# Block-diagonal queries and keys laid out by 24 small copies within SBUF for each batch, in place of masked products on POOL

## What is computed

```python
Q = (x @ Wq + bq).reshape(B, S, H, Hd)            # H = 16 heads, Hd = 16
K = (x @ Wk + bk).reshape(B, S, H, Hd)
scores = jnp.einsum('bqhd,bkhd->bhqk', Q, K) * scale + alibi
attn = softmax(scores, axis=-1)                   # self: over the keys
...
sm = jnp.einsum('nlhd,nshd->nlhs', q, k) / math.sqrt(D)
sm = softmax(sm, axis=1)                          # cross: over the queries
attn = jnp.einsum('nlhs,nshd->nlhd', sm, v)
...
x = layernorm(x + ffn(x))                         # quantised weights and activations
```

## Time and profile before

| | before |
|---|---|
| median of 3 runs | 1400.16 us (1396.43 to 1400.56) |
| the profiled execution, its own time | 1398.15 us |
| its span (first to last instruction) | 1396.4 us |
| PE busy | 1226.5 us (88%) |
| PE weight loads | 897.2 us (64%) |
| DVE busy | 1159.4 us (83%) |
| ACT busy | 859.7 us (62%) |
| POOL busy | 396.4 us (28%) |
| the core's 16 DMA engines | 24 GB/s mean |
| TensorE clock granted, mean | 0.966 of full |

### The profile page before, as it was taken

How to read it: one execution, slowest core, us unless ns; L and a number is a source line. 1 busy time by engine, 2 the same in 40 slices (tenths; PEclk the granted TensorE clock), 3 DMA queues, 4 the chain that set the end, 5 groups by cost and what they waited for, 6 DMA issues and landing times. The chain is left out here.

```text
span 1396.4 us, 28360 instructions
## 1 busy us (share of the span) xinstructions
PE 1226.5 (88%) x8850; PEld 897.2 (64%) x8850; DVE 1159.4 (83%) x2358; ACT 859.7 (62%) x2306; POOL 396.4 (28%) x463
## 2 busy tenths in 40 slices
PE   1689999999999999999999999999858878596776
PEld 1466666666666666666666666666527766496776
DVE  6369999999999999999999999999853468868787
ACT  2366666666666666666666666666424479786443
POOL 0233322234322234322234322233100000000887
PEclk9999999999999999999999999999969989798898
DMA  5100000000000000000000000000000000000222
GB/s 159 39 19 16 19 28 25 18 21 18 18 27 22 18 21 18 18 28 21 18 21 18 18 29 21 19 19 5 7 7 1 0 0 0 0 1 8 62 69 72
DMA packets 35042, 33.07 MB, mean 24 GB/s; under 512 B 4148, under 2 KB 34604, under 8 KB 34988
## 3 DMA queue, kind: packets, MB, share of 16 engines
q1 hardware_dynamic: 32704, 31.50, 7.3%
q10 hardware_dynamic: 2284, 0.89, 0.3%
HBM read 25.04 MB, written 7.34 MB: 23 GB/s over the span
## 5 line engine op out<-in xcount | busy, mean ns | idle before, releaser
L561 ACT ACTIVATE Px<-score 125x896 f32<-125x896 f32 x192 | 176.2, 918 | 128.1 <-PE score L1080 66.7
L747 DVE TENSOR_REDUCE nmax_c<-score 125x8 f32<-125x896 f32 x192 | 208.3, 1085 | 5.6 <-PE score L1002 5.1
L729 DVE TENSOR_REDUCE Zc<-Px 125x8 f32<-125x896 f32 x192 | 206.6, 1076 | 7.3 <-ACT Px L561 3.8
L554 ACT ACTIVATE Ps<-score,nmax_s 112x112 f32<-112x112 f32 x512 | 173.1, 377 | 3.9 <-DVE nmax_s L754 3.9
L506 POOL TENSOR_TENSOR rstd<-vare,half 112x1 f32<-112x1 f32 x64 | 35.1, 548 | 473.6 <-DVE vare L839 473.6
L1080 PE MATMUL score<-sel,nmaxT 128*125 128x448 f32 x384 | 125.1, 407 | 1.8 <-ACT nmaxT L567 1.8
L554 ACT ACTIVATION_READ_ACCUMULATOR Ps<-score,nmax_s 112x1 f32 x512 | 118.6, 232 | 0.0
L1091 PE MATMUL outX<-Px,Vn 125*32 125x224 f32 x1536 | 113.2, 368 | 2.5 <-DVE Vn L740 2.5
L740 DVE TENSOR_TENSOR Vn<-Vx,rZc 125x128 f32<-125x128 f32 x192 | 112.8, 588 | 1.2
L567 ACT ACTIVATE nmaxT<-maxT 128x125 fp32r<-128x125 f32 x192 | 53.5, 279 | 89.2 <-PE maxT L1074 88.9
L1002 PE MATMUL score<-Qbd_hi,KxT_hi 64*125 64x448 f32 x384 | 90.3, 466 | 1.2 <-ACT Px L561 1.2
(11 more groups left out here) (252 smaller groups left out, 3588.1 us busy)
## 6 DMA issues: line engine op xcount, KB each, us to landing
ctx_in<-in_ctx SPq DMA_DIRECT2D x32, 375.0 KB
x_in<-in_x SPq DMA_DIRECT2D x32, 112.0 KB, 2.0
x_scratch<-x SPq DMA_DIRECT2D x32, 112.0 KB, 5.4
x2T_all<-x_scratch SPq DMA_DIRECT2D x32, 112.0 KB, 2.0
out<-x2T_all SPq DMA_DIRECT2D x32, 112.0 KB, 1.9
raw_w_up<-in_w_up SPq DMA_DIRECT2D x1, 768.0 KB, 5.6
raw_w_down<-in_w_down SPq DMA_DIRECT2D x1, 768.0 KB, 7.2
raw_w_gate<-in_w_gate SPq DMA_DIRECT2D x1, 768.0 KB, 9.6
```

What stands on the lines that cost most here:

```text
L554: ins = act.activation(Ps[:, g, :], score[slot][0:L, h // QUAD, (h % QUAD) * L:(h % QUAD + 1) * L], ACT.Exp, bias=nmax_s[:, g:g + 1], accu ...
L561: act.activation(Px[u % 2][:].rearrange("s (q h) l -> s q (h l)", q=2), score[SLOT_OF[f"C{u}"]][0:C, :, 0:QW], ACT.Exp).then_inc(exp_c, 1)
L729: dve.tensor_reduce(Zc[p][:], Px[p][:], AX.X, ALU.add).then_inc(z_c, 1)
L747: dve.tensor_reduce(nmax_c[u % 2][:, 0:OCT].rearrange("s (q h) -> s q h", q=2), score[SLOT_OF[f"C{u}"]][0:C, :, 0:QW].rearrange("s q (h l) ...
```

## The change

The kernel after the change makes the same two layouts by plain copies from SBUF to SBUF, issued on SP's queue. One copy moves the 16 partitions of one head slot `(q, j)` to block `j`: for the keys both tiles and both parts at once (8 copies a batch, each 16 x 4 rows of 112 values), for the queries one tile with both parts (8 copies for each tile, each 16 x 2 rows of 112 values). Both tensors are cleared once at the start by POOL, and SP waits for that before its first load of the attention part. `Kbd` now exists twice (by parity of the batch); `Qbd` still exists once. `mask4` and POOL's products are gone. PE waits for all eight key copies of a batch before its first self scores, and for the eight query copies of tile `t` before the first unit of that tile. Source tensors of the high and the low part become halves of one tensor, which moves no work.

```diff
         @block.sync
+            def head_rows(q, j):
+                first = HALF_ROWS * q + HD * j
+                return slice(first, first + HD)
+
+            def diagonal_keys(n):
+                wait_drain(sp, (n, "Ks"))
+                for q in range(2):
+                    for j in range(QUAD):
+                        rows = head_rows(q, j)
+                        sp.dma_start(Kbd_both[n.par][rows, :, :, j].bitcast(F32).rearrange("r p t l -> r (p t) l"),
+                                     Ks_both[rows].bitcast(F32).rearrange("r p t l -> r (p t) l")).then_inc(kbd_done, 16)
+
+            def diagonal_queries(n, t):
+                if t == 0:
+                    wait_drain(sp, (n, "Qx"))
+                else:
+                    wait(sp, scores_c, n.times(NU))
+                for q in range(2):
+                    for j in range(QUAD):
+                        rows = head_rows(q, j)
+                        sp.dma_start(Qbd_both[rows, :, t, j].bitcast(F32), Qx_both[rows, :, t].bitcast(F32)).then_inc(qbd_done[t], 16)
+
+            sp.wait_ge(diagonal_cleared, 3)
+
             def step(n0, n1, n2, n3, n4, n5, n6):
+                if n4:
+                    diagonal_keys(n4)
+                if n2:
+                    diagonal_queries(n2, 0)
                 if n5:
                     load_x(n5)
+                if n2:
+                    diagonal_queries(n2, 1)
+                if n5:
                     load_ctx(n5)
                 if n0:
                     save_x2(n0)
...
         @block.gpsimd
+            for both in (*Kbd_both, Qbd_both):
+                pool.memset(both[:].bitcast(F32), 0.0).then_inc(diagonal_cleared, 1)
             pool.wait_ge(const_ld, constants.LOADED)
-            pool.tensor_tensor(mask4[:], mask8[:, 0:QUAD], mask8[:, QUAD:OCT], ALU.add).then_inc(mask_done, 1)
...
-            def block_diagonal(dst, src, t, done):
-
-                for h in range(2):
-                    ins = pool.tensor_tensor(
-                        dst[h][:, t],
-                        src[h][:, t:t + 1, :].bitcast(F32).broadcast_to([P, QUAD, L]),
-                        mask4[:].rearrange("p (h o) -> p h o", o=1).broadcast_to([P, QUAD, L]), ALU.mult)
-                ins.then_inc(done, 1)
...
             def step(n0, n1, n2, n3, n4, n5, n6):
                 if n5:
                     add_output_bias(n5)
-                if n4:
-                    diagonal_queries(n4, 0)
                 if n2:
                     inverse_root(n2, 1)
-                if n6:
-                    diagonal_keys(n6, 0)
-                    diagonal_keys(n6, 1)
-                if n4:
-                    diagonal_queries(n4, 1)
...
         @block.tensor
             def self_scores(n, t):
-                pe.wait_ge(kbd_done, n.times(KT, t + 1))
+                pe.wait_ge(kbd_done, n.times(HEADS_LAID, HEADS_LAID))
...
             def cross_scores(n, u):
                 if c == 0:
-                    pe.wait_ge(qbd_done, n.times(KT, t + 1))
+                    pe.wait_ge(qbd_done[t], n.times(HEADS_LAID, HEADS_LAID))
```

More of the change, by code:

```diff
@@ L37 @@
 HALF_ROWS = QUAD * HD
+HEADS_LAID = 16 * OCT
 BANK = 512
@@ L181, in __init__ @@
         mask8 = sb("mask8", [P, OCT])
-        mask4 = sb("mask4", [P, QUAD])
         even_odd = sb("even_odd", [P, 2])
@@ L344, in attention @@
         Vx = [sb(f"Vx{p}", [C, NC, D]) for p in range(2)]
-        Qx = [sb(f"Qx_{p}", [P, KT, L], F32R) for p in ("hi", "lo")]
-        Qbd = [sb(f"Qbd_{p}", [P, KT, QUAD, L], F32R) for p in ("hi", "lo")]
+        Qx_both = sb("Qx_both", [P, 2, KT, L], F32R)
+        Qx = [Qx_both[:, p] for p in range(2)]
+        Qbd_both = sb("Qbd_both", [P, 2, KT, QUAD, L], F32R)
+        Qbd = [Qbd_both[:, p] for p in range(2)]
         Qs = [sb(f"Qs_{p}", [P, KT, L], F32R) for p in ("hi", "lo")]
-        Ks = [sb(f"Ks_{p}", [P, KT, L], F32R) for p in ("hi", "lo")]
-        Kbd = [sb(f"Kbd_{p}", [P, KT, QUAD, L], F32R) for p in ("hi", "lo")]
+        Ks_both = sb("Ks_both", [P, 2, KT, L], F32R)
+        Ks = [Ks_both[:, p] for p in range(2)]
+        Kbd_both = [sb(f"Kbd_both{b}", [P, 2, KT, QUAD, L], F32R) for b in range(2)]
+        Kbd = [[both[:, p] for p in range(2)] for both in Kbd_both]
         xT = sb("xT", [P, KT, L])
@@ L395, in attention @@
         ctx_hi, kx_hi, ks_hi, qs_hi, qx_hi = (sem(n) for n in ("ctx_hi", "kx_hi", "ks_hi", "qs_hi", "qx_hi"))
-        kbd_done, qbd_done = sem("kbd_done"), sem("qbd_done")
+        kbd_done, qbd_done = sem("kbd_done"), [sem(f"qbd_done{t}") for t in range(KT)]
         scores_s, nmax_s_done, exp_s = sem("scores_s"), sem("nmax_s_done"), sem("exp_s")
@@ L476, in _ @@
             pool.memset(xmax_all[:], 0.0).then_inc(consts, 1)
+            for both in (*Kbd_both, Qbd_both):
+                pool.memset(both[:].bitcast(F32), 0.0).then_inc(diagonal_cleared, 1)
             pool.wait_ge(const_ld, constants.LOADED)
-            pool.tensor_tensor(mask4[:], mask8[:, 0:QUAD], mask8[:, QUAD:OCT], ALU.add).then_inc(mask_done, 1)
-            pool.wait_ge(mask_done, 1)
             pool.wait_ge(bo_folded, 1)
-            def block_diagonal(dst, src, t, done):
-                for h in range(2):
-                    ins = pool.tensor_tensor(
-                        dst[h][:, t],
-                        src[h][:, t:t + 1, :].bitcast(F32).broadcast_to([P, QUAD, L]),
-                        mask4[:].rearrange("p (h o) -> p h o", o=1).broadcast_to([P, QUAD, L]), ALU.mult)
-                ins.then_inc(done, 1)
-            def diagonal_keys(n, t):
-                if t == 0:
-                    wait_drain(pool, (n, "Ks"))
-                wait(pool, scores_s, n.back(1).times(KT, t + 1))
-                block_diagonal(Kbd, Ks, t, kbd_done)
-            def diagonal_queries(n, t):
-                if t == 0:
-                    wait_drain(pool, (n, "Qx"))
-                wait(pool, scores_c, n.back(1).times(NU, NC * (t + 1)))
-                block_diagonal(Qbd, Qx, t, qbd_done)
             def inverse_root(n, k):
@@ L581, in hi_keys_self @@
             def hi_keys_self(n):
-                wait(act, kbd_done, n.back(1).times(KT, KT))
+                wait(act, kbd_done, n.times(HEADS_LAID))
                 hi_with_bias(n, "Ks", Ks[0], bcol["abk"], ks_hi)
             def hi_queries_cross(n):
-                wait(act, qbd_done, n.back(1).times(KT, KT))
+                for t in range(KT):
+                    wait(act, qbd_done[t], n.times(HEADS_LAID))
                 hi_with_bias(n, "Qx", Qx[0], bcol["xbq"], qx_hi)
@@ L1059, in self_scores @@
                     pe.matmul(dst[:, q, 0:QW], alibi_l[rows], alibi_r[rows, t], start=True, stop=False)
-                row_halves(dst, Qs, Kbd, t, slice(0, L), False).then_inc(scores_s, 1)
+                row_halves(dst, Qs, Kbd[n.par], t, slice(0, L), False).then_inc(scores_s, 1)
             def cross_scores(n, u):
```

6 lines of the change are left out of this document (3 added, 3 removed).

## The result

The changed kernel takes 1525.72 us (median of 4 runs, 1520.91 to 1528.2), against 1399.3 us for the kernel before on the same chip. The ratio is 1.0902, with a 95% interval of 1.0868 to 1.0936: slower by 9%, where the prediction said 1377 us and faster. The profiled execution took 1520.91 us, its span is 1519.1 us, and the mean granted clock of TensorE fell from 0.966 to 0.929.

What follows compares the result with a forecast made beforehand. PE was taken to set the pace, busy 97.3 of 100 us, with DVE close behind. 1398.15 - 27 for the gain + 5.1 for start and end = 1376.3, set at 1377 for the runs' median; range 1350 to 1410.

Steps and rivals of the forecast that it cites:

- The gain: Attention part: without POOL's products PE's work after the maxima comes 1.0 us earlier a batch, 27 us in all.
- the second hold of `Vn`: DVE's operation on `Vn` at 500.47, lengthened beside POOL's products; surplus 1.38 us a batch, standing before PE's gap.
- PE's gap before the transpose: PE's largest idle time in the batch, 0.95 us before the transpose at 503.19, ended by DVE's `nmax_c`.
- the first hold: DVE's operation on `Vn` at 493.96, lengthened beside POOL's products; surplus 0.69 us a batch, priced at nothing.
- DVE isn't the pace: Denies the rival that DVE sets the pace, where both surpluses on `Vn` count and the time is 1347; chance 0.10.
- The landing: Time for an SBUF copy to land: 2.0 us taken, from loads that took 1.8 to 5.9.
- The issue: SP's time for each of 24 copies a batch: 0.37 us, bounds 0.36 and 0.48, taken from loads.
- The price of being late: PE's wait for late query copies, priced at the lateness times 31 batches; 1.6 us late gives 1426 us.
- The rival: The queries' tile-0 copies come late behind SP's eight key copies, so the kernel is slower; chance 0.21.
- What was priced at nothing in the steady state: Copies of keys and queries' tile 1, and the delayed `load_x`, `load_ctx` and `save_x2`: no cost, their buffers being wanted later.
- The start: Start of the attention part: first load 1.9 us late, first keys 1.2, first queries 1.0; with 1.0 at the end, 5.1.

Runs made afterwards that it cites:

- the floor: The changed kernel with only the first of the eight copies of each layout issued, 3 copies a batch in place of 24; 1369.51 us, ratio 0.9796.
- The probe: Kernel without the decoder's work, issuing groups of eight transfers, each after the last landed; a group took 4.98 to 5.11 us within SBUF, 3.55 to 3.63 with HBM.

## Why the prediction was wrong, step by step

**The gain: right.** I had 1.0 us a batch, from the second hold of `Vn` and PE's gap before the transpose. Three runs without late queries gave 1.02 (keys copied only), 1.08 (one copy of eight) and 1.00 us (POOL reordered). That the first hold is worth nothing is shown by the reordered POOL: one hold stays and the gain is whole. That DVE isn't the pace is shown by PE at 100 of 100 us.

**The landing: right.** 2.0 us taken, 1.8 and 2.0 measured.

**The issue: the step that failed.** "One copy costs SP 0.37 us, with 0.36 and 0.48 as bounds": it costs 0.64, outside both bounds. I took the bounds from loads from HBM and treated the issue as the same for any transfer. The probe shows that the two ends of the transfer set it, 0.59 against 0.42, and that even for loads the lone one that I read is the cheap case. Worked through with 0.64, my own arithmetic gives 490.84 + 15 x 0.64 + 1.8 = 502.2 for the last copy against PE's read at 499.34, 2.9 us late where I had 0.9 early; measured 3.12.

The estimate from the Trainium skill (DMA: Bandwidth & Descriptors, section Why a DMA increments its semaphore by 16 and not by 1), 0.427 us for an issue and 0.48 with the gap, lay just at that point, and I let a row on another kind of transfer overrule it. The probe agrees with it for loads (0.42 and 0.45), and it is too low for copies within SBUF (0.59 and 0.64).

**The price of being late: too low.** The rival had the mechanism and took lateness times 31. It is 4.4 us of time on the mean for 3.1 us of wait, since behind most of the waits TensorE's clock falls to 0.50: that is shown by the run in which six products keep PE at work and give 44 us back, and by the batches of the changed kernel in which the clock didn't fall. With waits of 0.6 to 0.8 us it fell behind none in the steady state, so the price isn't a fixed factor. From the floor: 1369.5 + 31 x 4.4 = 1506, and 8.4 later at the first maxima (96.2 against 87.8) make 1514; measured 1526.

The rest is in the filling and emptying of the pipeline. There single issues are longer still, as the rows of `Kbd_both` show for 110 to 280 us and for 280 to 920 (ns, min/median/max):

```profile
L474 SPq DMA_DIRECT2D Kbd_both<-Ks_both x40: 585/595/1845, 115.6 to 256.9; - x40
...
L474 SPq DMA_DIRECT2D Kbd_both<-Ks_both x158: 587/595/627, 285.7 to 919.5; - x158
```

Of all copies nine issues took 1.0 to 1.8 us, all before 280 or after 920 us. In eight batches there PE waits 3.5 to 4.3 us in place of 3.1, together 5.6 us more; its last two waits are 2.2 us shorter together. That leaves some 8 us that I didn't take apart.

**What was priced at nothing in the steady state: right.** Keys, tile 1, `load_x`, `load_ctx` and `save_x2`: the run with the keys copied and the one with the queries on POOL's queue have PE at 100 of 100 us, and in the changed kernel the copies of the queries are the only wait of PE's products from 400 to 700 us (27.3 us in nine waits).

**The start: too low by half.** 5.1 us for start and end; the start alone is 10.3, the end nothing behind the last maxima (14.1 us to the end of the part, 14.0 before). The clears cost 2.1 against 1.9, and the first transpose of `x_in` stands at 41.23 where I said 41, but by another way: the load was in time, and DVE was late, as told below. The first keys were late by 4.6 us, not 1.2, the first queries by 4.9, not 1.0: again eight and sixteen issues of 0.64.

## What to carry to other kernels

Price an issue by the kind of transfer, from a row with the same two ends and with others right behind it. If no row has it, the bound is open upwards, and the sum must be asked at which issue cost it turns: here that was 0.48 us, 0.11 above the value taken. Count what stands ahead in the same queue, since eight cheap copies are one long instruction for whatever comes ninth. And before work is moved off an engine because it holds another, see whether moving it in time does the same: POOL's other order gave 26 us for three moved lines and a second buffer, which were not tried apart.

A wait on PE that comes back in each batch can cost more than its length, by the clock that falls behind it: here 1.4 us on the mean for 3.1 us of wait, and nothing for 0.6 to 0.8. In such a place additional work can even be faster than none. And one batch is a thin sample: by luck the one read first was a middle one, with others 1.3 us shorter and 1.1 longer.

## What the hardware showed that I hadn't expected

A clear on POOL holds DVE. In the changed kernel POOL clears the two copies of `Kbd_both`, and DVE's scaling of a constant, 0.51 us before the change, takes 1.93 beside it; two operations on two values, 0.18 and 0.15 before, take 1.63 and 1.58. POOL's row, and DVE's:

```profile
33.23 3.63 POOL L513 MEMSET Kbd_both<- 128x1792 f32 x2
```

```profile
33.40 1.93 DVE L717 TENSOR_SCALAR xWq<-xWq 128x512 f32<-128x512 f32 x1
35.25 1.63 DVE L719 TENSOR_SCALAR abq<-abq 128x2 f32<-128x2 f32 x1
```

The two clears end near 35.05 and at 36.86, and the two operations of DVE's rows at 35.33 and 36.88: here DVE gets on when POOL changes from one instruction to the next. The Trainium skill (SBUF — State Buffer, section SBUF: two separate sides) describes a pair of ports that DVE and POOL lock for a whole instruction, the loser standing still. The trace agrees, here with 1.6 us for two values a partition, and in the shorter of the held `Vn`, which ends at 494.93, 0.15 us after POOL's product at 493.85. The longer one goes beyond it: it starts at 500.47, beside one product, and ends at 502.14, after the next one too (501.05 to 501.98), so it didn't get on when POOL changed.
